# Depthwise causal convolution behind an attention layer: three bf16 parts and taps that stay on chip

## The reference

```python
def _L1_cond_ref(x, w, b):          # x (16, 512, 1024), w (16, 1, 1024), b (1024,)
    K = w.shape[0]
    D = x.shape[-1]
    y = jax.lax.conv_general_dilated(x, w, window_strides=(1,), padding=[(K - 1, 0)],
                                     feature_group_count=D, dimension_numbers=('NWC', 'WIO', 'NWC'))
    return y + b
x = x + _L0_cond_ref(x, cond_2048, Wq, Wo)
x = x + _L1_cond_ref(x, cond_2048[:, None, :], L1_cond_b)
```

## Time and profile before

| | |
|---|---|
| median of three runs | 4569.91 us (4569.88 to 4571.38) |
| profiled execution | 4572.62 us, of which the span from the first to the last instruction is 4570.9 us |
| convolution, its first instruction to the end of the span | 4074.05 to 4570.9 us |
| first and last matmul work of the convolution | 4119.58 and about 4561.9 us |
| TensorE, share of the span busy | 96% |
| mean granted clock of TensorE, as a share of 2.4 GHz | 0.940 |

### The profile page before, as it was taken

How to read it: one execution, slowest core, us unless ns; L and a number is a source line. 1 busy time by engine, 2 the same in 40 slices (tenths; PEclk the granted TensorE clock), 3 DMA queues, 4 the chain that set the end, 5 groups by cost and what they waited for, 6 DMA issues and landing times. The chain is left out here.

```text
span 4570.9 us, 54681 instructions
## 1 busy us (share of the span) xinstructions
PE 4372.5 (96%) x17536; PEld 3215.0 (70%) x17536; DVE 2754.8 (60%) x2405; ACT 2849.6 (62%) x3777; POOL 2606.2 (57%) x1044
## 2 busy tenths in 40 slices
PE   6999999999999999999999999999999999949999
PEld 4776767676766767676767676676767676729999
DVE  4665646565555556565655555565656565619998
ACT  4776757576766767576767667675757676722332
POOL 3775757575666757575757667575757576620000
PEclk8999999999999999999999999999999999975555
DMA  3324223333323232232333232323323332233442
GB/s 97 79 65 102 66 57 87 74 88 79 91 69 81 66 102 66 69 88 69 86 79 88 70 81 68 97 66 78 82 68 84 79 88 70 60 122 126 148 157 83
DMA packets 205368, 385.70 MB, mean 84 GB/s; under 512 B 17960, under 2 KB 119976, under 8 KB 205096
## 3 DMA queue, kind: packets, MB, share of 16 engines
q1 hardware_dynamic: 205096, 382.08, 32.1%
HBM read 112.79 MB, written 67.11 MB: 39 GB/s over the span
## 5 line engine op out<-in xcount | busy, mean ns | idle before, releaser
L579 POOL TENSOR_TENSOR plo<-p,phi 128x1024 fp32r<-128x1024 f32 x1024 | 2600.5, 2551 | 1422.2 <-ACT phi L529 1411.7
L622 DVE TENSOR_REDUCE mrow<-misc 128x1 f32<-128x1024 f32 x1024 | 1214.9, 1217 | 1082.3 <-PE misc L373 1078.2
L527 ACT ACTIVATE p<-sc 128x512 f32<-128x512 f32 x2048 | 1110.6, 594 | 854.9 <-PE sc L410 605.2
L423 PE MATMUL pv<-phi,val 128*128 128x512 f32 x4096 | 1139.4, 400 | 41.5 <-issue 41.5
L529 ACT ACTIVATE phi<-p 128x1024 fp32r<-128x1024 f32 x1024 | 1086.0, 1061 | 32.5
L423 PEld LDWEIGHTS pv<-phi,val 128*128 128x128 f32 x4096 | 769.1, 189 | 249.4 <-issue 76.1
L409 PE MATMUL sc<-quer,keys 128*128 128x512 f32 x2048 | 919.5, 449 | 24.2 <-issue 18.8
L410 PE MATMUL sc<-quer,keys 96*128 96x512 f32 x2048 | 815.7, 398 | 0.0
L427 PE MATMUL pv<-plo,val 128*128 128x512 f32 x2048 | 648.6, 398 | 0.7 <-POOL plo L579 0.7
L373 PE MATMUL misc<-quer,keys 128*128 128x512 f32 x2048 | 596.5, 399 | 22.7 <-DMA keys<-lo 11.6
L409 PEld LDWEIGHTS sc<-quer,keys 128*128 128x128 f32 x2048 | 387.6, 189 | 202.0 <-issue 76.4
(11 more groups left out here) (49 smaller groups left out, 3319.4 us busy)
## 6 DMA issues: line engine op xcount, KB each, us to landing
keys<-hi SPq DMA_DIRECT2D x256, 256.0 KB, 3.1
quer<-mhi SPq DMA_DIRECT2D x256, 256.0 KB, 4.4
xb<-x SPq DMA_DIRECT2D x16, 2048.0 KB, 8.8
keys<-lo SPq DMA_DIRECT2D x128, 256.0 KB, 4.9
quer<-mlo SPq DMA_DIRECT2D x128, 256.0 KB, 3.8
xo<-x SPq DMA_DIRECT2D x64, 512.0 KB, 4.1
x<-xo SPq DMA_DIRECT2D x64, 512.0 KB, 5.3
xin<-x SPq DMA_DIRECT2D x8, 4096.0 KB, 19.9
```

What stands on the lines that cost most here:

```text
L423: pe.matmul(pv[:, half(h)], val[:, i, t, part, :], phi[:, t % NPHI, half(h)], start=(t == 0 and part == 0), stop=False)
L527: act.activation(p32[:, t % NP32, half(h)], sc[:, h, :], ACT.Exp, scale=SCALE).then_inc(s_p32, 1)
L579: pool.tensor_tensor(plo[:, t % NPLO, :], p32[:, t % NP32, :], phi[:, t % NPHI, :].bitcast(F32), ALU.subtract).then_inc(s_plo, 1)
L622: reduced = dve.tensor_reduce(mrow[:, q:q + 1], misc[:, k, :], AX.X, ALU.max)
```

## The change

**Taps.** The host lays the taps out already rotated and by partition (`tap_rows`), so that one DMA brings them. VectorE adds the diagonal, multiplies them with two small triangles `tri` (one per matrix) into a bf16 tile, and then places them: `place_taps(h, g)` multiplies a half of the positions (64 of 128) with a scalar per partition that is 1 in group g and 0 elsewhere, and so writes the 16 columns of group g of both matrices. All matrices of all 128 positions then stay on chip in `toep`, bf16, for the four rounds. The first half is placed before the first chunk, the second during the first eight chunks.

**x1 in three parts.** ScalarE copies a chunk of x1 to bf16 (`first_part`), VectorE subtracts it from x1 into float32 (`rest`), of which the upper 16 bits are taken as they lie as the second part, and subtracts those again into bf16 (`last_part`). All three have the positions innermost (8), so that the writes are packed and a weight load takes every 8th bf16 (every 16th in the middle part). A position takes six matmuls instead of four.

**Bias.** It is split into three bf16 rows on three partitions of an otherwise zero tile `brow`, and comes into each bank with a matmul of 512 columns ahead of the others.

**Eviction.** ScalarE copies the banks to `stage`; VectorE has no part in it. ScalarE's order is: both evictions of chunk k, then the first part of chunk k+2.

**Halves.** x1 is laid out as (16, 512, 16, 64), so that a load brings half of the tokens of 4 batches (4 MB in two DMAs, pieces of 1 KB instead of 2 KB), and `store_xo` writes pieces of 64 floats, 256 bytes. The load of the half after next is issued behind every second store of results.

```diff
             def store_xo(b, m):
-                             xo[:, m % 2, :].rearrange("p (g n) -> p g n", n=TG)).then_inc(s_xo_out[m % 2], 16)
+                             xo[:, m % 2, :].rearrange("p (g n) -> p g n", n=TH)).then_inc(s_xo_out[m % 2], 16)
...
-        toep = sb("toep", [P, 2, 2, TC, P], F32R)
-        taps = sb("taps_sb", [P, CH, TG], BF16)
+        toep = sb("toep", [P, 2, TG, P], BF16)
+        taps = sb("taps_sb", [P, 2, TG, CH], BF16)
-        brow = sb("brow", [P, T], F32)
-        xin = sb("xin", [P, 2, SLOTS, TG], F32)
-        xh = sb("xh", [P, 2, TC, SLOTS], F32R)
-        xl = sb("xl", [P, 2, TC, SLOTS], F32R)
+        brow = sb("brow", [P, T], BF16)
+        pick = sb("pick", [P, P], BF16)
+        xin = sb("xin", [P, 2, SLOTS, TH], F32)
+        rest = sb("rest", [P, 2, SLOTS, TC], F32)
+        first_part = sb("first_part", [P, 2, SLOTS, TC], BF16)
+        last_part = sb("last_part", [P, 2, SLOTS, TC], BF16)
...
+        def upper(a):
+            return a.bitcast(BF16)[..., 1::2]
...
-            load(0)
-            for l in range(CH):
-                t = taps_in.rearrange("k (g n) -> g k n", n=TG)
-                sp.dma_start(taps_f32[l:P:CH, l:CH, :], t[:, 0:CH - l, :]).then_inc(s_taps, 16)
-                if l:
-                    sp.dma_start(taps_f32[l:P:CH, 0:l, :], t[:, CH - l:CH, :]).then_inc(s_taps, 16)
+            sp.dma_start(taps_f32, taps_in).then_inc(s_taps, 16)
+            load(0)
...
+            for k in range(ROUNDS * STAGES):
+                store(k)
+                if k % 2 == 1 and k // 2 + 2 < 2 * ROUNDS:
+                    load(k // 2 + 2)
...
         @block.scalar
-            for k in range(ALL):
-                high(k)
+            def evict(n):
...
+                act.wait_ge(s_bank, n + 1)
+                act.activation(stage[:, s % 2, :, to:to + PER_BANK * NG].rearrange("p l (n g) -> p l n g", g=NG),
+                               acc[n % NBANK][:].rearrange("p (n g l) -> p l n g", n=PER_BANK, l=CH),
+                               ACT.Copy).then_inc(s_res, 1)
+            first(0)
+            first(1)
+            for k in range(ALL):
+                for f in range(FILLS):
+                    evict(FILLS * k + f)
+                if k + 2 < ALL:
+                    first(k + 2)
         @block.vector
+            def place_taps(h, g):
+                for w in range(2):
+                    dve.tensor_scalar(toep[:, w, h * TH:(h + 1) * TH, g * CH:(g + 1) * CH],
+                                      taps[:, w, h * TH:(h + 1) * TH, :], group[:, g:g + 1], None,
+                                      ALU.mult).then_inc(s_toep, 1)
+            def parts(k):
+                dve.wait_ge(s_first, k + 1)
+                dve.tensor_tensor(rest[:, k % 2], raw(k), first_part[:, k % 2], ALU.subtract).then_inc(s_rest, 1)
+                dve.wait_ge(s_rest, k + 1)
+                dve.tensor_tensor(last_part[:, k % 2], rest[:, k % 2], upper(rest[:, k % 2]), ALU.subtract).then_inc(s_last, 1)
...
+            for g in range(NG):
+                place_taps(0, g)
+            bias_rows()
+            for k in range(ALL):
+                parts(k)
+                if k < PER_LOAD:
+                    place_taps(1, k)
         @block.tensor
...
+                slabs = (first_part[:, k % 2], upper(rest[:, k % 2]), last_part[:, k % 2])
                 for f in range(FILLS):
...
+                    extra = brow[:, n0:n0 + PER_BANK * NG].unsqueeze(2).to_broadcast([P, PER_BANK * NG, CH])
+                    pe.matmul(acc[at % NBANK][:], pick[:], extra, start=True, stop=False, skip_group_check=True)
                     for i in range(PER_BANK):
...
-                        pe.matmul(o, hi[:, NB:SLOTS], t0, start=True, stop=False)
-                        pe.matmul(o, hi[:, 0:P], t1, start=False, stop=False)
-                        pe.matmul(o, lo[:, NB:SLOTS], t0, start=False, stop=False)
-                        last = pe.matmul(o, lo[:, 0:P], t1, start=False, stop=True)
+                        for slab in slabs:
+                            pe.matmul(o, slab[:, NB:SLOTS, j], t0, start=False, stop=False, skip_group_check=True)
+                            last = pe.matmul(o, slab[:, 0:P, j], t1, start=False, stop=slab is slabs[-1],
+                                             skip_group_check=True)
```

More of the change, by code:

```diff
@@ L767, in build_conv, with load @@
         block = ctx.enter_context(nc.Block())
-        N_TAPS = 16 * (2 * CH - 1)
         ALL = ROUNDS * CHUNKS
+        ROWS = (0, 32, 64)
         out_rows = out.rearrange("b (c l) t -> b c l t", l=CH)
+        def upper(a):
+            return a.bitcast(BF16)[..., 1::2]
         @block.sync
         def _(sp):
[L775 to L780, removed]
+            def load(i):
+                r, h = i // 2, i % 2
+                src = x1[h * NG:(h + 1) * NG, :, r * NB:(r + 1) * NB, :].rearrange("g (l c) b n -> (g l) c (b n)", l=CH)
+                dst = xin[:, h].rearrange("p (c b) n -> p c (b n)", b=NB)
+                for part in range(2):
+                    c = slice(part * NC // 2, (part + 1) * NC // 2)
+                    sp.dma_start(dst[:, 1 + c.start:1 + c.stop, :], src[:, c, :]).then_inc(s_in[h], 16)
             def store(k):
@@ L846, in _, with first @@
         def _(act):
-            def high(k):
-                if k % CHUNKS == 0:
-                    act.wait_ge(s_in[k // CHUNKS % 2], 32 * (k // CHUNKS // 2 + 1))
+            def first(k):
+                if k % PER_LOAD == 0:
+                    act.wait_ge(s_in[k // PER_LOAD % 2], 32 * (k // CHUNKS + 1))
                     act.wait_ge(s_zero, 2)
@@ L860, in _ @@
+            dve.memset(pick[:], 0.0).then_inc(s_brow, 1)
+            dve.memset(brow[:], 0.0).then_inc(s_brow, 1)
+            dve.wait_ge(s_brow, 2)
+            for row in ROWS:
+                dve.memset(pick[row:row + 1, :], 1.0).then_inc(s_brow, 1)
             dve.wait_ge(s_keep, 7)
             dve.tensor_reduce(own[:], eye[:].rearrange("p (g l) -> p l g", l=CH), AX.X, ALU.max).then_inc(s_own, 1)
-            dve.wait_ge(s_own, 1)
-            dve.wait_ge(s_taps, N_TAPS)
-            dve.tensor_tensor(taps[:], taps_f32, own[:].unsqueeze(2).to_broadcast([P, CH, TG]), ALU.add).then_inc(s_own, 1)
@@ L893, in _ @@
-            for k in range(2):
-                build_taps(k)
-                low(k)
+            dve.tensor_reduce(tri[:], keep[:].rearrange("p w (g l) -> p w l g", l=CH), AX.X, ALU.max).then_inc(s_own, 1)
+            dve.tensor_reduce(group[:], eye[:].rearrange("p (g l) -> p g l", l=CH), AX.X, ALU.max).then_inc(s_own, 1)
+            dve.wait_ge(s_own, 3)
+            dve.wait_ge(s_taps, 16)
+            own_b = own[:].unsqueeze(1).to_broadcast([P, TG, CH])
+            dve.tensor_tensor(taps_f32, taps_f32, own_b, ALU.add).then_inc(s_own, 1)
@@ L896, in _ @@
+            dve.wait_ge(s_own, 4)
+            for w in range(2):
+                tri_b = tri[:, w:w + 1, :].to_broadcast([P, TG, CH])
+                dve.tensor_tensor(taps[:, w], taps_f32, tri_b, ALU.mult).then_inc(s_own, 1)
+            dve.wait_ge(s_own, 6)
+            for g in range(NG):
+                place_taps(0, g)
+            bias_rows()
             for k in range(ALL):
-                results(k)
-                if k + 2 < ALL:
-                    build_taps(k + 2)
-                    low(k + 2)
+                parts(k)
+                if k < PER_LOAD:
+                    place_taps(1, k)
@@ L938, in by_group, with tap_rows @@
     a = np.asarray(a)
[L939 removed]
+    halves = a.reshape(*a.shape[:-1], 2, TH, NG)
+    return np.ascontiguousarray(np.swapaxes(halves, -1, -2).reshape(a.shape))
+def tap_rows(cond):
+    back = np.asarray(cond)[::-1].reshape(CH, TG, NG)
+    l = np.arange(CH)
+    return np.ascontiguousarray(back[(l[None, :] - l[:, None]) % CH].transpose(3, 0, 2, 1).reshape(P, TG, CH))
 def kernel(x, cond_2048, L0_cond_Wq, L0_cond_Wo, L1_cond_b):
```

98 lines of the change are left out of this document (43 added, 55 removed).

## The result

The changed kernel takes 4359.55 us, the median of four runs (4359.01 to 4360.27), against 4569.90 us (4568.05 to 4571.38) for the kernel before on the same chip: a ratio of 0.954 with a 95% interval of 0.9523 to 0.9557. Forecast were 4405 us and a range of 4365 to 4565. The direction and the mechanism held; the time lies 45 us under the forecast and 5.5 us under the range. The profiled execution took 4359.2 us for a span of 4357.5 us.

The account below looks back on a forecast made before the run. TensorE and VectorE were both taken to fill the convolution's chunks at 1.2 GHz. First matmul at 4109.5, plus 285 (chunks), 3 (low-clock start) and 9.0 (tail) gave 4406.5, so a 4405 us median; own range 4365 to 4435, overall to 4565.

Parts of the forecast that it names:

- The circle: Convolution, two buffers: chunk k+2 waits for chunk k's evictions, then copy and two subtractions; 4.7 us per turn.
- (L + T) / 2: Convolution: the period per chunk is the larger of T and this; about 4.45 us taken.
- L: Convolution: time from the end of a chunk on TensorE until the chunk after next can start; 4.7 us.
- T: Convolution: TensorE's own time for a chunk; 3.25 to 4.26 us at the high clock, 4.26 taken.
- the size of a pair: Convolution: one bf16 weight load and 128-column matmul; 0.058 to 0.079 us at 2.4 GHz, 0.107 to 0.127 at 1.2 GHz.
- the transposes of line 380: Value transposes with 128-column loads and 128 moving columns in another mode; 0.079 us each, taken as nearest row for a pair.
- the preparation: Before the convolution's first matmul: taps, products, placements, bias rows, first parts; first matmul at 4109.5 (4104 to 4122), against 4119.6.
- the stores that I had priced: End of the attention: two 256-byte-piece stores of x1, with two reloads between, on the path; 4 us added (0 to 12).
- the lower end: Whole kernel: 4.0 us per chunk and first matmul at 4104 give 4370 us; range starts at 4365.
- The low clock: Rival, convolution: TensorE stays at 1.2 GHz; 4502 us, or 4560 at 6.9 us per chunk; chance 0.20, including a pair in between.
- strided weights: Rival, convolution: weight loads with a step take two cycles per column; 11.1 us per chunk, 4828 us; chance 0.18.
- The three rows that the prediction names for the rival: Lines 853, 874 and 870: about 2.0 ns per element with a step, against 1.0 to 1.2 packed.

Follow-up runs that it names:

- e1: Changed kernel with three buffers instead of two for the three parts of x1: 4328.51 us, ratio 0.947 to the kernel before.
- e2: Changed kernel with ScalarE's copy for chunk k+2 ahead of the second eviction of chunk k: 4345.23 us, ratio 0.9507 to the kernel before.
- e3: Changed kernel with the x1 parts laid out as before, slots innermost, so weight loads are packed and writes have a step: 4542.32 us.
- e6: Kernel before with bf16 instead of float32r for the matrices and both x1 parts, third part left out: 4726.8 us, ratio 1.0342.
- e9: Changed kernel with two float32r pairs (zero weights) added ahead of the six bf16 pairs of each position: 4468.0 us, ratio 0.9777 to the kernel before.
- e5: Kernel before with the eviction moved to ScalarE, bias left out: 4564.04 us, ratio 0.9989.
- e7: Kernel before with both bf16 operands (third part left out) and eviction by ScalarE (bias left out): 4649.3 us, ratio 1.0175.
- e4: Changed kernel without ScalarE's copy, first part read in place from x1's float32 tile, 256 bytes between weight columns: 4388.34 us, ratio 0.9604.
- e8: Changed kernel with three buffers for the parts and the bias rows made by GpSimd instead of VectorE: 4330.84 us, ratio 0.9471 to the kernel before.

## Why the prediction was wrong in its time and right in its mechanism

**Right.** The clock rose 2.9 us behind the first matmul and stayed at 1.00. All durations named for ScalarE and VectorE hold within 0.02 us (1077, 600, 1258 ns for 1.09, 0.6, 1.25). The circle was described as it is, with the rule (L + T) / 2, which e1 and e2 confirm to about 1 us. TensorE idles on the last part, 0.34 us per chunk by its record ((54.2 - 32.3) / 64, without the wait for the first chunk), where 0.2 stood. The transfers cost nothing at this period (DMA share 0.70 over the chunks, and no wait for a load between 4110 and 4350), the 256-byte stores nothing (5.1 us to landing against 5.3 before, 166.7 us of waiting against 175.2), and the tail took 9.1 us for 9.0.

**Wrong: the size of a pair, and with it T.** "I take T = 4.26, as the transpose is the nearest row" is the step that failed. The pair takes 0.061 to 0.063 us, near the lower of the two bounds given (0.058), and the transposes of line 380 (0.079) were no measure of it. They are matmuls in another mode, and the 512-column matmuls of the trace had shown that one column per cycle is reached. T is 3.4 instead of 4.26 us, which by the rule is 0.43 us per chunk. L is 4.42 instead of 4.7, and that is 0.14: the copy starts 0.49 us behind the eviction where 0.69 was allowed, and the other hand-overs are 0.03 to 0.05 us instead of 0.1, while the signal at the end of the chunk takes 0.2 instead of 0.1. Together this is 64 x 0.57 = 37 us, the distance between 250.7 us and the 285 and 3 that stood there. That it comes out so exactly is luck: the 4.45 of the sum is 4.48 rounded down, worth 2 us, and of the 3 us for the first chunks less than 1 is seen (the first takes 4.65 us). The Trainium skill ("TensorE: Matmul & The Clock Gate", Back-to-back issue gap), with about 81 ns for such a pair, was cited beside this step; the measurement decides for 61 to 63, and 56 for packed weights.

**Wrong: the preparation, by 11.8 us.** The stage began at 4071.5 instead of 4078: 4 of these 6.5 us are the stores that I had priced, and 2.6 are no effect of the change. The start scatters: it lies between 4070.0 and 4076.9 in the nine kernels with the new stores and between 4068.5 and 4074.1 in the four with the old ones, so that a cost of the stores up to about 2 us would not be seen. Sixteen placements took 6.4 us instead of 9.6: 0.40 us each, near the lower bound of 0.35, where I took 0.6. The taps landed 0.9 us earlier, the bias rows took 5.2 instead of 6. The terms named for the preparation add up to 4109.1, not 4109.5.

**Wrong: the lower end.** The range took 4.0 us per chunk and 4104 from the bounds, 4370 in all, and only 5 us more. Measured were 3.92 and 4097.7, 5 and 6 us less. The 4.0 already had the pair at its lower bound; what was missing is that L had bounds of its own (0.3 us under the value taken). And 4104 is not the sum of the low bounds given: with stores at nothing and placements at 0.35 us the terms add up to 4101.

**The sum.** The chunks (37 us) and the preparation (12) make 49 us from 4406.5 to the span of 4357.5. The distance of the times is only 45 us, since the forecast took 1.5 us off the span and the measured median lies 2 us above it: the execution profiled before the change was 2.7 us slower than the median of its kernel, and that offset was carried over.

**The rivals.** The low clock is ruled out by the first chunk, in which the clock rises. Of "strided weights" it holds that a step is not free (5 to 6 ns of 56 at 16 or 32 bytes, 58 ns at 256 bytes), but the forecast loss would need a pair of 0.125 us at the low clock, and it was 0.107, the bound given for one column per cycle. The rule of the Trainium skill ("SBUF — State Buffer", Door 1), by which the result would have been this rival's, is not confirmed at these steps for TensorE. Of the three rows that the prediction names for the rival, line 870 has its step in what it reads and writes packed; 853 and 874 are writes. A step costs much where an engine writes with it, and bf16 pays more than double of float32r (e3, e6). Had the change kept the layout of before, it would have stood at 4542 us.

**Open.** Why a four-byte write with a step of 528 bytes takes 2.1 us and a bf16 write with 264 bytes 4.8 to 5.1 isn't told apart here: element size and step in bytes changed together. Nor was a weight load with a step between 32 and 256 bytes tried. Why the clock rose is argued in the prediction and not isolated: the rows show it at 0.50 for 442 us of float32r pairs with TensorE busy throughout, at 1.00 from 2.9 us behind the first bf16 chunk's start, and at 1.00 too with 16 float32r pairs in each chunk among the others (e9); no run has float32r pairs alone in the new order of work.

## What to carry to other kernels

When two engines are full, relieving one shows almost nothing (e5), and relieving the other can lose when its operands become dearer to write (e6): look for the layout that makes both light, and price a step in a write with the type that will be written. In a double-buffered chain the period is (L + T) / 2 as long as that exceeds T; read L and T off the timeline, and weigh a third buffer (31 us here) against a shorter chain (14 us). Where a duration is bounded from both sides, take the bound whose mechanism the trace shows at work, and let the low end of the range hold all terms at their low bounds together.

## What the runs showed that I had not expected

- bf16 writes of 1056 elements with a step of 132 elements: 4812 and 4878 ns on ScalarE, 5138 on VectorE (and 5420 in e7); float32r with the same count and step in elements: 2159 and 2152.
- Float32r pairs of 128 columns cost 0.137 us among bf16 pairs at 2.4 GHz and 0.213 at 1.2 GHz; bf16 pairs 0.061 and 0.107.
- A weight load with 256 bytes between columns makes a pair mostly 0.11 to 0.15 us at 2.4 GHz, and in the same kernel VectorE's unchanged subtraction takes 1868 ns instead of 1258 (e4).
- Five instructions of GpSimd on a single partition each, and VectorE's products and placements beside them take 6.3 us longer (e8).
- In e3, in the stretch shown, TensorE stood still for 4.7 us and the granted clock was 0.50 behind it until the microsecond from 4209; the mean over the middle was 0.87. In the changed kernel, with waits of up to 0.9 us in a chunk, it stayed at 1.00.
